# Four graph layers on one core: when the rows of x W are stored, and which loads stand behind those stores

## The reference

```python
# layer 0, the only one that the change touches
xw  = x @ W                       # 6250 x 128
ew  = edge_attr @ edge_w          # 206250 x 16 times 16 x 128
msg = xw[src] * ew
x   = layernorm(x + segment_sum(msg, dst) + b)
# layers 1 to 3: mean, degree-normalised and gated aggregation over the same edges,
# each followed by x = layernorm(x + ...)
```

## Time and profile before

| what | value |
|---|---|
| runs, median of 3 | 2834.29 us |
| span of the profiled execution | 3281.4 us |
| PE, DVE, POOL, ACT busy | 71%, 48%, 50%, 15% of the span |
| POOL L722, the gathers | 1612, 1527.1 us busy, 954.7 us idle before them |
| mean DMA rate | 139 GB/s |

### The profile page before, as it was taken

One profiled execution on the slowest core, in us unless ns is written; L12 is line 12 of the kernel. 1 busy time (PEld: TensorE's weight loads), 2 busy tenths in 40 slices (PEclk: granted clock), 3 DMA queues, 4 the chain that ended last, 5 costly groups with the idle time before them and its releaser, 6 DMA issues.

```text
span 3281.4 us, 35388 instructions
## 1 busy us (share of the span) xinstructions
PE 2326.1 (71%) x13074; PEld 1466.3 (45%) x13074; DVE 1559.3 (48%) x2576; ACT 497.8 (15%) x798; POOL 1652.8 (50%) x1762
## 2 busy tenths in 40 slices
PE   3566656666666666667666567666677989999996
PEld 2344444444444444444444344444444544455553
DVE  2555554555554555555555555555554531222126
ACT  1011111111111111111111111111111221111113
POOL 5566656656666666656666656656664110002212
PEclk6556556566666776777777777777777999999998
DMA  6223232323333343433344344444445988876661
GB/s 203 57 86 87 82 88 84 106 84 92 107 96 99 101 122 95 120 100 110 113 135 114 106 116 121 136 121 132 119 128 120 245 294 306 291 268 247 248 242 40
DMA packets 456700, 456.22 MB, mean 139 GB/s; under 512 B 163573, under 2 KB 402250, under 8 KB 456522
## 3 DMA queue, kind: packets, MB, share of 16 engines
q1 hardware_dynamic: 237358, 281.24, 25.7%
q0 software_dynamic: 52832, 109.16, 12.5%
q10 hardware_dynamic: 166332, 63.48, 8.0%
HBM read 368.61 MB, written 85.13 MB: 138 GB/s over the span
## 4 chain that ended last, share of the span: by engine, by line
another core or an unknown queue 46%; PE 35%; ACT 7%; issue 7%; DVE 2%; DMA 2%; SPq 0%; ACTq 0%; POOL 0%; DVEq 0%; POOLq 0%
PE pb L1509 8%; PE pb L1510 8%; ACT tmp L1636 7%; PE pb L1378 5%; PE pb L1405 4%; PE pb L1368 2%; PE pb L1384 2%; PE pb L1326 2%; PE pb L1437 2%; PE pb L1527 1%; DMA big<-at 1%; DMA tmp<-at 0%; ACTq L1642 0%; ACT big L1670 0%
## 5 line engine op out<-in xcount | busy, mean ns | idle before, releaser
L722 POOL DMA_INDIRECT big<-xw,big x1612 | 1527.1, 947 | 954.7 <-issue 580.0
L909 DVE TENSOR_TENSOR big<-pb,big 128x512 f32<-128x512 f32 x404 | 260.0, 685 | 1073.1 <-remote 683.2
L1378 PE MATMUL pb<-big 128*128 128x98 f16 x3136 | 272.9, 248 | 643.2 <-ACT tmp L1636 562.1
L1405 PEld LDWEIGHTS pb<-big 128*128 128x128 f32 x3232 | 546.2, 258 | 349.1 <-issue 334.1
L1405 PE MATMUL pb<-big 128*128 128x64 f32 x3232 | 584.1, 346 | 124.4 <-issue 119.6
L1636 ACT CAST tmp<-pb 128x784 f16<-128x784 f32 x392 | 318.3, 812 | 2043.0 <-remote 1628.5
L1378 PEld LDWEIGHTS pb<-big 128*128 128x128 f16 x3136 | 231.9, 124 | 726.5 <-issue 405.6
L835 DVE TENSOR_TENSOR big<-pb,big 128x2048 f16<-128x2048 f32 x196 | 447.5, 2283 | 0.8
L1326 PE MATMUL pb<-big 64*128 64x512 f32 x808 | 327.3, 898 | 108.4 <-DVE big L909 83.7
L837 DVE TENSOR_TENSOR big<-pb,big 128x1568 f16<-128x1568 f32 x196 | 348.8, 1780 | 0.0
L1384 PE MATMUL pb<-tmp,ident 128*128 128x392 f16 x784 | 239.1, 446 | 0.0
(11 more groups left out here) (231 smaller groups left out, 1600.0 us busy)
## 6 DMA issues: line engine op xcount, KB each, us to landing
at<-tmp SPq DMA_DIRECT2D x196, 392.0 KB
big<-at SPq DMA_DIRECT2D x24, 3200.0 KB, 10.9
big<-at SPq DMA_DIRECT2D x24, 3072.0 KB, 19.7
big<-at ACTq DMA_DIRECT2D x32, 896.0 KB
big<-xw,big POOLq DMA_INDIRECT x1612
big<-in_ea SPq DMA_DIRECT2D x202, 64.0 KB
big<-at SPq DMA_DIRECT2D x13, 896.0 KB
big<-at ACTq DMA_DIRECT2D x24, 336.0 KB
```

The costliest lines, as they stand in the source:

```text
L722: nc.gpsimd.indirect_dma_start(gath[:, T8 * (n % NG) + t % T8, :], None, xw_d, bass.IndirectOffsetOnAxis(ap=src_i[:, t:t + 1], axis=0)).th ...
L909: nc.vector.tensor_tensor(msg[:, T8 * (n % 2) + 4 * q:T8 * (n % 2) + 4 * q + 4, :], PB[:, q, :].rearrange("p (t f) -> p t f", f=D), gath[: ...
L1378: last = nc.tensor.matmul(PB[:, 4 + g, i * KW:i * KW + KW], hot_lo[:, at_pair, :], hot_key[:, at_pair, :], start=True, stop=True)
L1405: last = nc.tensor.matmul(PB[:, 2 + n % 2, 0:WIN], msg[:, T8 * (n % 2) + t, :], hot_win[:, T8 * (n % 2) + t, :], start=(t == 0), stop=(t = ...
```

## The change

The stores of x W get seven rooms instead of four: the four of `gath`, two in the buffer of the messages (`msg`), and one in that of the one-hot keys (`hot_key`). The copies on ScalarE lose their wait for a store. On SyncE the loop over the seven stores moves up to stand right behind the loads of xT; the load of `src` goes between the third and the fourth store, and the other loads stand behind the seventh. VectorE gets a wait for all seven stores ahead of its first one-hot matrix.

```diff
-        xwS = gath
+        xw_rooms = [gath[:, T8 * t:T8 * t + BT, :] for t in range(4)] + [msg[:, T8 * t:T8 * t + BT, :] for t in range(2)]
+        xw_rooms.append(hot_key.rearrange("p t f -> p (t f)")[:, 0:2 * BT * D].bitcast(F32).rearrange("p (t f) -> p t f", f=D))
...
                 sp.dma_start(xT[:, c0:c1], xT_d[:, c0:c1]).then_inc(s_in[f"xT{part_of}"], 16)
+            for t in range(NT):
+                sp.wait_ge(s_rowev, 2 * t + 2)
+                sp.dma_start(xw_d[t * BT * P:(t + 1) * BT * P, :].rearrange("(b p) f -> p b f", p=P), xw_rooms[t]).then_inc(s_rowst[t % 4], 16)
+                if t == 2:
+                    sp.dma_start(src_i, src_d).then_inc(s_in["src"], 16)
+                if t == NT - 2:
+                    sp.wait_ge(s_first, 2)
+                    sp.dma_start(first_d.rearrange("(p b) o -> p (b o)", b=NPB), run_edge[:, :]).then_inc(s_run, 16)
             sp.dma_start(wts[:, 1:7, :], w_d[1:7].rearrange("w k n -> k w n")).then_inc(s_in["w"], 16)
...
-            sp.dma_start(src_i, src_d).then_inc(s_in["src"], 16)
...
-            for t in range(NT):
-                sp.wait_ge(s_rowev, 2 * t + 2)
-                sp.dma_start(xw_d[t * BT * P:(t + 1) * BT * P, :].rearrange("(b p) f -> p b f", p=P),
-                             xwS[:, T8 * (t % 4):T8 * (t % 4) + BT, :]).then_inc(s_rowst[t % 4], 16)
-                if t == NT - 2:
-                    sp.wait_ge(s_first, 2)
-                    sp.dma_start(first_d.rearrange("(p b) o -> p (b o)", b=NPB), run_edge[:, :]).then_inc(s_run, 16)
             sp.wait_ge(s_run, 16)
...
+            for h in range(4):
+                v.wait_ge(s_rowst[h], 16 * ((NT + 3 - h) // 4))
             window_hot(0)
...
-                    if t >= 4 and q == 0:
-
-                        act.wait_ge(s_rowst[t % 4], 16 * (t // 4))
-                    nc.scalar.copy(xwS[:, T8 * (t % 4) + 4 * q:T8 * (t % 4) + 4 * q + nb, :], PB[:, 2 * (t % 2) + q, 0:nb * P].rearrange("p (b n) -> p b n", n=P)).then_inc(s_rowev, 1)
+                    nc.scalar.copy(xw_rooms[t][:, 4 * q:4 * q + nb, :], PB[:, 2 * (t % 2) + q, 0:nb * P].rearrange("p (b n) -> p b n", n=P)).then_inc(s_rowev, 1)
```

## The result

The changed kernel takes 2843.4 us, the median of six runs (2840.47 to 2847.09); the kernel before takes 2834.47 in runs beside them. The ratio is 1.003 with a 95% interval of 1.0019 to 1.0042. It is slower by about 9 us: inside the predicted range near its upper end, and 7.4 us above the forecast of 2836.

A forecast was written before the change was run, and what follows sets the result against it. GpSimd's gathers were the costliest group, but whether they or TensorE's wait set the pace was left open. The middle of −2.9 and +4.9 us, taken as about +1.5 on 2834.29, gave 2836 us; range 2828 to 2845.

The forecast's parts named there:

- the long wait: Rival: `first_edge` served number by number between packets of x, GpSimd loses 18 us at `slots_in(0)`; 2850 us; chance 0.12.
- the two lines of the sum: End moves with group 0 on VectorE (−2.9 us) or with `slots_in(0)` on GpSimd (+4.9 us); middle taken, about +1.5.
- The head start: Seventh store goes out near 24.4 instead of 27.32, so GpSimd's first gather starts at 29.5, 2.9 us earlier.
- The wait at `slots_in(0)`: GpSimd waits for `first_edge`, issued at 34.8 and landing 9.2 us later; start at 45.0, in the runs 4.9 us later.
- The spacing of gathers in the runs: GpSimd's gathers taken to come every 1.25 us in the profile and about every 0.96 us in the runs.
- Which line carries: Whether TensorE's wait (end moves −2.9 us) or GpSimd (+4.9 us) sets the pace; undecided, middle about +1.5 us.
- the wait on TensorE at group 2: In the first profile VectorE starts group 2 35.7 us behind TensorE's recorded sums of group 1; left unexplained.
- Group 0: VectorE's start on group 0, 47.78 before, comes 2.9 us earlier, with its moved inputs just hidden, cover about 2 us.
- 22.6 us of its ceiling: At `slots_in(0)`: each engine's 200 numbers of `first_edge` let one packet of x pass each, 113 ns apiece; landing near 57.4.
- the whole head start: Rival: `first_edge` lands before GpSimd asks, first gather near 26, 6.4 us earlier; 2828 us; chance 0.2.
- Nothing comes through: Rival: the long wait for TensorE at group 2 is tied to something that doesn't move; 2834.3 us; chance 0.15.
- the 0.22: Chance given to a measurably slower kernel: 0.1 from the forecast's upper end plus 0.12 from the long wait.

The follow-up runs named there:

- the second profile of before: The kernel before, unedited, profiled again: 2835.65 us (one run); first gather at 31.85, `slots_in(0)` at 41.85, group 6 at 94.3.
- the early bias: Changed kernel with `first_edge` loaded right behind the seventh store and the bias loaded ahead of the stores: 2832.58 us, 0.999 of the kernel before.
- `first_edge` early: Changed kernel with the wait for `run_edge` and the load of `first_edge` moved right behind the seventh store: 2836.59 us, 1.0003 of the kernel before.

## Why the prediction held in its range, and which steps of it failed

The change came out slower, as forecast, but by 8.9 us and not by 1.5, and above the forecast's own bounds (2831.4 to 2839.2). It lies in the range because that took in half of the long wait. The sign owes something to luck: it came from the +4.9 us of a spacing that is wrong. With the spacing that the runs have, the two lines of the sum are −2.9 and +2.6, and their middle is next to nothing. The middle of −2.9 and +4.9 is besides +1.0, not the +1.5 that I took.

*The head start* held. The first gather was forecast at 29.5 and started at 28.14; the seventh store at 24.4 and went out at 23.85, behind L787 as said. It landed 3.3 us later and not 4.06, the emptier queue that the text allowed for. Measured against the second profile of before (31.85) the head start is 3.7 us.

*The wait at `slots_in(0)`* held as a mechanism, and its size was too small. `first_edge` was issued at 33.90 (34.8 forecast), but took 16.9 us, not 9.2. The 9.2 came from the fifth `ea`, which stood behind one load of 128 rows of 6464 bytes. Those went one for one with packets of x too (86 to 87 from 35 to 37 us in the second profile of before), so it is the number of packets that counts, not their size. Here 640 rows of 512 bytes stood ahead in the list, and the 3200 numbers went one for one as well while x lasted. Holding back x took the 16.9 down to 4.2. So L705 started at 51.58, not 45.0. This is the term that failed most.

*The spacing of gathers in the runs* was wrong. I took 0.96 us because the profiled execution was 447 us longer than the runs. The second profile of before has the length of the runs and still 1.25 us. With 1.25 the move of L705 for 45.0 would have been +2.6, and for the measured 51.58 it is +9.2 (+9.7 against the second profile).

*Which line carries.* I took the middle between group 0 on VectorE and L705 on GpSimd. The runs show GpSimd alone: group 0 did not move (47.78) and the end moved by 8.9 us. In the table the time follows the start of group 6 within 2 us in every kernel: +9.7 and +8.9 for the changed one, −2.2 and −3.0 for the early bias, each against the kernel before. The ground for the middle was the wait on TensorE at group 2, and that wait is not in the kernel.

*Group 0* was to gain 2.9 us, with the moved inputs just hidden. The inputs were hidden: VectorE and TensorE had the first edge products done by 42. The gathers ate the gain. I saw the fill of `yT` move beside the first gathers and priced its own time only. It holds a gather up by 2.85 us, and L791 another by 0.9; hidden behind the wait for `first_edge`, this cost nothing in the changed kernel, and it is what kept "`first_edge` early" from its gain.

*The rivals.* The long wait has the right sign, the right place and half of its mechanism. The numbers of `first_edge` did go one by one between packets of x, but only from 43 to 45 us; then x ran out, so that they never cost the 22.6 us of its ceiling. The rows ahead of them, which it left out, took the larger part. The 6.4 us of the whole head start were seen in no run: with `first_edge` and the bias moved too the kernel was some 3 us faster than before, barely clear of the noise. "Nothing comes through" fell with the wait at group 2. The chances put 0.58 on no change that can be told; the result lies in the 0.22.

## What to carry to other kernels

When loads are moved behind something, look for the smallest of them that another engine's list waits for, count the packets (rows, or single numbers) ahead of it and in it, and ask what will be in flight on the other queues when it goes out. Here a load of 12.5 KB decided, and cost more than twice the head start. Where one engine paces a long loop, follow that engine's list to its first wait: here a change ahead of the loop was worth about what it did to that engine's start in it. A profile that is much longer than the runs should be taken again before its waits are argued from.

## What the runs showed of the hardware that was not expected

- Two queues in use at once took turns by packets, one for one whatever their size: 86 of q1 to 87 of q10 with rows of 6464 bytes (second profile of before, 35 to 37 us), 413 to 408 with rows of 512 (changed kernel, 38 to 42 us), 234 to 224 with single numbers of 4 bytes (43 to 45 us). So the queue with the 512-byte rows got 0.19 of 1.03 MB. From 34 to 38 us it was one to two (246 to 491), and that stays open.
- An indirect DMA that starts on GpSimd beside a 3.5 to 3.7 us copy of VectorE takes 3.8 to 4.0 us instead of 0.95, and beside a 1.84 us `tensor_tensor` with two inputs in SBUF 1.8 to 2.5 us. Beside a 1.78 us one with an input in PSUM it takes 0.94.
- One profiled execution of the kernel before was 16% longer than its runs, with gaps such as the 35.7 us between TensorE's recorded sums of group 1 and VectorE's start on group 2, and a mean granted clock of 0.752 against 0.793; a second had the length of the runs. No cause was found.
